# Attention products in one set of 512 columns a unit, key maxima turned in blocks, row sums moved by transfers

## The chip, the cores and the metric

The kernel runs on one core of one Trainium2 chip. The metric is the device time of one execution in microseconds (us). A core has TensorE (PE; its weight loads are shown as PEld), VectorE (DVE), ScalarE (ACT), GpSimd (POOL) and SyncE (SP), each with a program of its own; they meet at semaphores. SP, here, does little but start transfers (DMA); its queue is shown as SPq.

## The reference, cut to what matters

A macaron block on x of 8 x 512 x 128 values in float32: an attention and mixture-of-experts half, an RWKV-6 recurrence, and the same half again, each added to x.

```python
x = x + 0.5 * ffn(layernorm(x))     # "first mixer" and "first experts"
x = x + rwkv6(layernorm(x))
x = x + 0.5 * ffn(layernorm(x))     # "second mixer" and "second experts"

def ffn(x):                                            # 8 batches of 512 tokens, 128 channels
    h = layernorm(x) * w + b
    q, k, v = heads(h @ w_qkv)                         # 16 heads of 8 channels
    p = softmax(q @ k.T / sqrt(8))                     # 512 x 512 for every head and batch
    x = x + (p @ v) @ w_proj
    h2 = layernorm(x)
    return x + expert_mlp[argmax(h2 @ gate_w + gate_b)](h2)
```

The change lies in the attention and in the choice of the expert; the recurrence and the experts' own products are as they were.

## The kernel before, in words

`mixer_phase` does the attention half and the routing; it is called twice. For each of 8 batches `b` there are 4 steps `g` of four heads (a group), numbered G = 4 b + g. A step has 4 units `u` of 128 keys; 128 units in a mixer. A unit of group G holds:

- on TensorE four **scores** of group G + 2 (`score`, L652: queries in rows, all keys in 512 columns), from which VectorE takes the maxima over the keys;
- four **exponent products** of group G (`exponent`, L660: keys in rows, queries in columns; the maxima stand as extra rows of the stacked operand `q_stack`, so that the product comes out with the maximum taken off), which ScalarE turns into `probs` by Exp (L933);
- the **value products** of the unit before it (`pv`, L670: four matmuls of 32 output columns, one a head, side by side in the array; each over half of the 512 queries, so two sets of four a unit);
- and at some units one of the other jobs of a batch, by the rules of `jobs` (turning with the identity, the q, k and v projections, the output projection, the gate, the ranks).

Score and exponent product of one place are called a pair below; their operands lie in opposite halves of the array's rows. Two of TensorE's results go through small sets of PSUM banks: the scores through 4 banks (two pairs of heads; `reduce_pair`, L986, reads two banks at once and `s_read` frees them), the exponent products and all jobs in turn through a ring of 3 banks (`RINGS = 3`, `ring_free`: an instruction waits until the third user before it has been read). Every engine takes its instructions in the order written.

The maxima go from VectorE to GpSimd (`split_max`, split in a high and a low part), are turned by TensorE (`turn_max`, L679), copied by ScalarE (`keep_rows`), and written to the rows of `q_stack` by SP (`place`). The sums of the probabilities come out of the value products as a ninth column. At the end of two groups the sum bank is copied (`keep_o`), turned (`turn_o`), copied (`copy_o`), the sums inverted on VectorE (`invert`), multiplied on GpSimd (`normalize`), and the whole turned back once a batch (`turn_y`, `keep_y`) for `project`.

Before the first unit come the statistics, q, k and v of two batches, SP's stores of their split parts to memory and loads into the stacks of a group (12 transfers a group, `load_group`), and the scores of groups 0 and 1. After the last unit come the rest of the last batch's chain (output projection, norm, gate, rank, scatter of the rows to the experts' order) and 8 transfers of padding rows.

Of the kernel before, what the change touches and what calls it, by code (L numbers as in the profile page):

```python
# [5 lines left out]
F32 = mybir.dt.float32  # L6
# [186 lines left out]
def load_constants(nc, ctx, d, x_all, padding, xs):  # L193
# [14 lines left out]
    routing = [(sb("w_proj", [P, P]), d["L0_ffn_w_proj"]),  # L208
# [31 lines left out]

    def load_late(sp, part):
# [17 lines left out]
    with nc.Block() as block:  # L259
        @block.sync  # L260
        def _(sp):
            for dst, src in first:
                sp.dma_start(dst[:], src).then_inc(loaded, 16)
            for j in range(SL):
                here = slice(j * ST, (j + 1) * ST)
                sp.dma_start(x_all[:, here, :], x_slices[:, here, :]).then_inc(s["x_loaded"][j], 16)
            for dst, src in routing:
                sp.dma_start(dst[:], src).then_inc(s["routing_loaded"], 16)
# [14 lines left out]
    return s, load_late, wait_rest  # L283
# [14 lines left out]
def mixer_phase(nc, ps, s, x_all, z_all, rows, expert, first_row, xs, qd, kd, load=None):  # L298
    with Phase(nc) as ctx:
# [6 lines left out]
        def sbs(name, shape, dt=F32):  # L306
            return [sb(f"{name}{i}", shape, dt) for i in range(2)]

        y_all = rows[:, :, 0:P]
# [3 lines left out]
        spread, scales, power = sbs("spread", [P, 2, ST]), sbs("scales", [P, 2, ST]), sb("power", [P, 2, ST])  # L313
        zn, hT = sb("zn", [P, ST, P]), sb("hT", [P, SW])
# [9 lines left out]
        maxima = sbs("maxima", [P, 2, PAIRS, TPB])  # L324
        NMAX = 2 * SPLITS * PAIRS * TPB
        neg_wide = sb("neg_wide", [P, P], F32R)
        neg_parts = neg_wide[:, 0:NMAX].rearrange("p (e a m) -> p e a m", e=2, a=SPLITS)
        max_rows = sbs("max_rows", [P, P], F32R)
        oT = sb("oT", [P, T])
        o_rows, inv = sb("o_rows", [P, TPB, GROUP, SHARE, DK + 1]), sb("inv", [P, TPB, GROUP, SHARE])  # L330

        yT, h2T, x1 = sb("yT", [P, SW]), sb("h2T", [P, SW]), sb("x1", [P, ST, P])
# [15 lines left out]
            sem("power_set"), sem("ones_set"), sem("normed"), sem("z_made"), sem("turned"), sem("h_ready"))  # L348
        made = {k: sem(k + "_made") for k in "qkv"}
# [10 lines left out]
        split_step, split_done, rows_turned, rows_kept, rows_placed = (  # L360
            sem("split_step"), sem("split_done"), sem("rows_turned"), sem("rows_kept"), sem("rows_placed"))
        o_kept, o_turned, o_copied, inv_ready, o_done = (
            sem("o_kept"), sem("o_turned"), sem("o_copied"), sem("inv_ready"), sem("o_done"))

        numbered, y_turned, y_kept, projected = sem("numbered"), sem("y_turned"), sem("y_kept"), sem("projected")
# [5 lines left out]
        scattered, padded = sem("scattered"), sem("padded")  # L371
# [5 lines left out]
        PER_LOAD = 16 * 12  # L377
# [8 lines left out]
        def jobs(b, g, u):  # L386

            here = []
            if u == 1 and g % SHARE == 0 and (b or g):
                here.append(("o", shared(b, g)))  # L390
            if u == 1 and NG * b + g < LAST:
                here.append(("m", NG * b + g + 1))
            if b >= 2 and (g, u) == (0, 0):
                here.append(("gate", b - 2))
            if b >= 2 and (g, u) == (0, 2):
                here.append(("rank", b - 2))
            if b >= 1 and (g, u) == (1, 0):
                here.append(("turn_y", b - 1))
            if b + 2 < B and (g, u) == (1, 2):
                here.append(("turn_z", b + 2))  # L400
            if b >= 1 and (g, u) == (1, 3):
                here.append(("project", b - 1))
            if b + 2 < B and (g, u) == (2, 0):
                here.append(("q", b + 2))
            if b + 2 < B and (g, u) == (2, 2):
                here.append(("k", b + 2))
            if b >= 1 and (g, u) == (3, 0):
                here.append(("turn_h", b - 1))
            if b + 2 < B and (g, u) == (3, 2):
                here.append(("v", b + 2))  # L410
            if b == B - 1 and (g, u) == (3, 2):
# [1661 lines left out]
```

## Time and profile before

| | us |
|---|---|
| median of 3 runs (lowest, highest) | 1472.45 (1472.34, 1479.55) |
| the profiled execution: its time, its span | 1473.18, 1471.4 |
| TensorE busy over the span | 1230.9 (84%) |
| VectorE busy | 1042.9 (71%) |
| ScalarE busy | 860.7 (58%) |
| GpSimd busy | 553.6 (38%) |
| first mixer, from the first statistics to the experts' first load | 13.0 to 493.2 |

Busy time is the union of an engine's instructions. The profile shows the end of a matmul by a model, so two that follow each other overlap a little; the distance between starts is what a product costs the engine. A timeline row merges neighbouring instructions of one line: its first number is the start of the first, its second the time to the end of the last, xN their number (a matmul of float32 operands of L670, L699, L705 counts as two), and the bracket the idle time before it, with what ended it.

### The profile page before, as it was taken

How to read it: one execution, taken by the hardware profiler on the slowest of the kernel's cores; microseconds unless marked ns; L12 is line 12 of the kernel's file. 1: busy time of each engine (PE TensorE's matmuls, PEld its weight loads, DVE VectorE, ACT ScalarE, POOL GpSimd, SP SyncE). 2: the span in 40 equal slices, each digit the busy share in tenths (PEclk: the TensorE clock that was granted, in tenths of full speed). 3: DMA queues.
4: the chain of work that ended last, by engine and by line, in shares of the span. 5: the costliest groups of instructions: out<-in, count | busy, mean ns of one | idle time of the engine just before them, and what ended most of it. 6: DMA issues, size and time to landing. Idle time of an engine off the chain costs nothing. (4 is left out here: it accounts for less than half of the span.)

```text
span 1471.4 us, 36051 instructions
## 1 busy us (share of the span) xinstructions
PE 1230.9 (84%) x12512; PEld 661.3 (45%) x12513; DVE 1042.9 (71%) x1842; ACT 860.7 (58%) x1742; POOL 553.6 (38%) x797
## 2 busy tenths in 40 slices
PE   2799999999997596398888754999999999993893
PEld 1234444444443596145455442344444444442893
DVE  3889988988992332478788745888898988963232
ACT  2288877778775353444334411588788778881451
POOL 6122324323212354355676536222332431222462
PEclk9599999999999799599999955799999999996896
DMA  4322442222110121100000003122122122100224
GB/s 117 71 74 74 130 121 68 82 71 73 55 36 9 53 67 47 42 2 3 3 2 2 3 1 87 57 75 65 49 82 73 53 81 66 56 15 30 56 66 122
DMA packets 81540, 82.40 MB, mean 56 GB/s; under 512 B 16249, under 2 KB 53724, under 8 KB 81392
## 3 DMA queue, kind: packets, MB, share of 16 engines
q1 hardware_dynamic: 72560, 69.88, 16.7%
q0 software_dynamic: 4608, 8.44, 1.8%
q10 hardware_dynamic: 4224, 2.10, 0.5%
q8 instruction: 94, 1.54, 0.4%
q14 instruction: 54, 0.44, 0.1%
HBM read 50.42 MB, written 29.93 MB: 55 GB/s over the span
## 5 line engine op out<-in xcount | busy, mean ns | idle before, releaser
L986 DVE TENSOR_REDUCE maxima<-ps 128x2 f32<-128x1024 f32 x512 | 616.2, 1222 | 89.8 <-PE ps L652 88.5
L933 ACT ACTIVATE probs<-ps 128x512 f32<-128x512 f32 x1024 | 550.8, 600 | 120.3 <-PE ps L660 109.7
L652 PE MATMUL ps<-k_stack,q_stack 62*128 62x512 f32 x1024 | 390.0, 473 | 39.0 <-DVE maxima L986 21.7
L660 PE MATMUL ps<-q_stack,k_stack 64*128 64x512 f32 x1024 | 396.3, 464 | 4.2 <-ACT q_whole L869 3.4
L670 PE MATMUL ps<-probs,v_stack 128*32 128x256 f32 x4096 | 329.6, 394 | 0.9 <-ACT probs L933 0.4
L652 PEld LDWEIGHTS ps<-k_stack,q_stack 62*128 62x128 f32 x1024 | 160.1, 194 | 235.9 <-issue 138.3
L660 PEld LDWEIGHTS ps<-q_stack,k_stack 64*128 64x128 f32 x1024 | 159.2, 187 | 30.5 <-ACT q_whole L869 8.6
L670 PEld LDWEIGHTS ps<-probs,v_stack 128*32 128x32 f32 x4096 | 81.7, 108 | 166.6 <-issue 148.3
L532 POOL CAST neg_wide<-maxima 128x16 fp32r<-128x16 f32 x64 | 12.6, 196 | 286.7 <-DVE maxima L986 286.7
L1299 POOL DMA_INDIRECT expert_out<-yt,number x80 | 78.3, 979 | 72.4 <-POOL number L1295 44.1
L1276 DVE COPY w_now<-w 128x512 f32 x80 | 34.6, 433 | 80.1 <-issue 42.2
L1234 PE MATMUL ps<-xT,w_now 128*128 128x128 f32 x640 | 89.7, 285 | 0.2
L1241 PE MATMUL ps<-w,hidT 128*128 x640 | 84.7, 276 | 0.0
L1234 PEld LDWEIGHTS ps<-xT,w_now 128*128 128x128 f32 x640 | 80.9, 198 | 3.0 <-issue 2.4
L1257 ACT ACTIVATE xT<-ps,ln_b,ln_w 128x128 f32<-128x128 f32 x80 | 36.6, 457 | 73.1 <-PE ps L1228 73.1
L1241 PEld LDWEIGHTS ps<-w,hidT 128*128 128x128 f32 x640 | 78.2, 193 | 0.1
L558 POOL DMA_INDIRECT sorted<-rows,slot x64 | 63.6, 994 | 37.8 <-issue 20.8
L542 POOL TENSOR_TENSOR rows<-o_rows,inv 128x128 f32<-128x128 f32 x64 | 30.8, 501 | 122.1 <-DVE inv L993 122.1
L1262 ACT ACTIVATE hidT<-ps 128x512 f32<-128x512 f32 x80 | 47.8, 597 | 40.3 <-PE ps L1234 39.8
L1731 POOL TENSOR_TENSOR r_kx<-r_kx,r_k_factor 128x512 f32<-128x512 f32 x48 | 61.6, 1284 | 9.8 <-PE ps L1909 6.4
L1712 POOL TENSOR_TENSOR r_mixed<-r_shift,zT 128x512 f32<-128x512 f32 x40 | 58.7, 1474 | 16.0 <-DVE r_shift L1588 16.0
L1281 DVE COPY yt<-ps 128x128 f32<-128x128 f32 x80 | 23.3, 291 | 48.8 <-PE ps L1241 48.1
(208 smaller groups left out, 1622.7 us busy)
## 6 DMA issues: line engine op xcount, KB each, us to landing
q_stack<-q_split SPq DMA_DIRECT2D x256, 64.0 KB
k_stack<-k_split SPq DMA_DIRECT2D x512, 32.0 KB
q_split<-q_parts SPq DMA_DIRECT2D x16, 512.0 KB, 2.7
k_split<-k_parts SPq DMA_DIRECT2D x16, 512.0 KB, 3.6
xt<-sorted SPq DMA_DIRECT2D x80, 64.5 KB
w<-in_L_ffn_w SPq DMA_DIRECT2D x16, 256.0 KB, 3.0
rows<-expert_out SPq DMA_DIRECT2D x16, 256.0 KB, 4.5
x_all<-in_L_attn_x SPq DMA_DIRECT2D x8, 256.0 KB, 5.1
```

The lines of the kernel that those rows point to most:

```text
L558: pool.indirect_dma_start(xs, bass.IndirectOffsetOnAxis(ap=slot[:, i:i + 1], axis=0), rows[:, i, :], None).then_inc(scattered, 16)
L652: mm = t.matmul(psS[:, h, :], qs[g][score_rows(h), h // 2, u * P:(u + 1) * P], ks[g][score_rows(h), h // 2, :], start=True, stop=True)
L660: t.matmul(ring("e", G, u, n), ks[G % NG][half(h), h // 2, u * P:(u + 1) * P], qs[G % NG][half(h), h // 2, :], start=True, stop=True).then ...
L670: last = t.matmul(psO[VW * h:VW * (h + 1), here], vs[g][:, u, h, :], probs[u % 2][:, h, here], start=(g % SHARE == 0 and u == 0 and part = ...
L933: a.activation(probs[u % 2][:, h, :], ring("e", G, u, n), ACT.Exp, scale=float(DK) ** -0.5).then_inc(e_read, 1)
L986: v.tensor_reduce(maxima[G % 2][:, :, pair, u:u + 1], psS[:, 2 * pair:2 * pair + 2, :], AX_X, ALU.max, negate=True).then_inc(s_read, 1)
L1234: last = t.matmul(psH[o][:, c * P:(c + 1) * P], w1_now[o][:, c * P:(c + 1) * P], xT[o][:], start=True, stop=True)
L1241: last = t.matmul(psY[i][:, 0:P], hidT[i][:, c, :], s["w2"][:, ds(second_expert, 1), c, :], start=(c == 0), stop=(c == HC - 1))
L1262: a.activation(hidT[o][:].rearrange("p c t -> p (c t)"), psH[o], ACT.Gelu_apprx_tanh).then_inc(hidT_kept, 1)
L1299: pool.indirect_dma_start(ys, bass.IndirectOffsetOnAxis(ap=number[out_slot][:], axis=0), yt[out_slot][:], None, bounds_check=TOK - 1, oob_ ...
L1712: g.tensor_tensor(mixed[f][:], shift[f % 2][:], x, ALU.add).then_inc(mixed_ready.sem, 1)
L1731: g.tensor_tensor(dst[:].rearrange("p (k m) -> p k m", m=m), src[:].rearrange("p (k m) -> p k m", m=m), k_factor[l][:].rearrange("p n two ...
```

## The change

**Value products.** One set of four matmuls over all 512 queries, behind all four pairs of the unit, in place of two sets of 256 behind two pairs each.

**Maxima.** VectorE turns the 128 x 32 maxima in 32 x 32 blocks itself (`turn_maxima`); GpSimd splits the result; SP writes two images to memory and reads them back into `q_stack`. `turn_max` and `keep_rows` are gone from TensorE and ScalarE.

**Sums.** `oT` keeps the value products as they come. SP moves the sum rows to a 128 x 32 tile, VectorE inverts them, SP writes them to memory and reads them back repeated over the rows (`inv_wide`), GpSimd multiplies. `turn_o`, `copy_o`, `turn_y`, `keep_y` are gone; `project` runs over two halves of rows, 8 matmuls in place of 4.

**Norms.** The first norm's second scaling and the row norm move from VectorE to ScalarE in two units each (with scale and bias); `halve` moves from VectorE to GpSimd; the latter's 4 scalings become 2 operations over 512 columns.

**Transfers.** 4 loads a group of 32 rows in place of 12; q and k are stored in four transfers in place of two (the same parts twice). In the first mixer only two slices of x are loaded ahead, the rest and the routing constants from inside the phase. The padding rows go half from SP, half from ScalarE.

**Places.** The jobs stand at other units (`jobs`), and the last batch but one's gate and rank come behind the last unit.

```diff
 def jobs(b, g, u):
-    if u == 1 and g % SHARE == 0 and (b or g):
-        here.append(("o", shared(b, g)))
-    if u == 1 and NG * b + g < LAST:
-        here.append(("m", NG * b + g + 1))
-    if b >= 2 and (g, u) == (0, 0):
+    if b >= 2 and (g, u) == (0, 1):
+        here.append(("turn_h", b - 2))
+    if b >= 2 and (g, u) == (0, 3):
         here.append(("gate", b - 2))
...
+AFTER = [(k, B - 2) for k in ("turn_h", "gate", "rank")] + [(k, B - 1) for k in ("project", "turn_h", "gate", "rank")]
...
-def pv(unit, part):
+def pv(unit):
     g, u = unit // TPB % NG, unit % TPB
-    if part == 0:
-        pe.wait_ge(e_read, 4 * unit + 4)
-    here = slice(part * T // 2, (part + 1) * T // 2)
+    pe.wait_ge(e_read, 4 * unit + 4)
     for h in range(GROUP):
-        last = t.matmul(psO[VW * h:VW * (h + 1), here], vs[g][:, u, h, :], probs[u % 2][:, h, here],
+        last = t.matmul(psO[VW * h:VW * (h + 1), :], vs[g][:, u, h, :], probs[u % 2][:, h, :],
...
-                        if ahead:
-                            score(G + 2, u, 0)
-                        exponent(G, u, 0)
...
-                        values(1)
+                        for n in range(GROUP):
+                            if ahead:
+                                score(G + 2, u, n)
+                            exponent(G, u, n)
...
+                        if unit:
+                            pv(unit - 1)
...
 def project(p):
+    pe.wait_ge(o_done, NG // SHARE * (p + 1))
     for q in range(ST):
+        for n in range(NG // SHARE):
+            last = t.matmul(ring("project", p)[:, q * P:(q + 1) * P], yT[n][:, q * P:(q + 1) * P], s["w_proj"][:, n, :],
+                            start=(n == 0), stop=(n == NG // SHARE - 1))
...
+def turn_maxima(G):                       # VectorE
+    v.transpose(max_turned[:], maxima_wide[G % 2][:]).then_inc(max_blocks, 1)
...
+def place(G):                             # SP
+    image = max_images[G % 2]
+    for a, ready in enumerate((split_step, split_done)):
+        sp.wait_ge(ready, G + 1)
+        sp.dma_start(image[a].rearrange("c k q -> k c q"), neg_parts[:, a, :].bitcast(F32)).then_inc(max_stored, 16)
+    sp.wait_ge(max_stored, STORED * (G + 1))
+    for e in range(2):
+        sp.dma_start(qs[G % NG][at:at + SPLITS, :, :].bitcast(F32),
+                     image[:, e * count:(e + 1) * count]).then_inc(rows_placed, 16)
...
+def move_sums(count):                     # SP
+    sp.wait_ge(o_kept, count)
+    sp.dma_start(sums[:], oT[DK::OW, :]).then_inc(sums_moved, 16)
+def store_inv(count):
+    sp.wait_ge(inv_ready, count)
+    sp.dma_start(inv_image.rearrange("r (k q) -> (r k) q", q=BLOCK), inv[:]).then_inc(inv_stored, 16)
+def spread_inv(count):
+    sp.wait_ge(inv_stored, 16 * count)
+    sp.dma_start(inv_wide[:], inv_image.unsqueeze(1).broadcast_to([P // OW, OW, T])).then_inc(inv_spread, 16)
...
+def norm_second(j, tiles):                # ScalarE; norm_rows likewise, at (3, 2) and (3, 3)
+    for q in tiles:
+        last = a.activation(zn[:, q, :], x_all[:, j * ST + q, :], ACT.Identity, bias=shift[j % 2][:, q:q + 1],
+                            scale=scales[j % 2][:, 1, q:q + 1])
...
-for e in range(E):
+for e in range(E // 2):                   # padding rows on SP; the other half on ScalarE
```

On TensorE, one whole unit before, in the middle of the first mixer (L652 is a score, L660 an exponent product, L670 the value products of the unit before; a job, where there is one, follows the last row):

```order
L652 MATMUL ps<-k_stack_175,q_stack_171 128x512
L660 MATMUL ps<-q_stack_169,k_stack_173 128x512
L652 MATMUL ps<-k_stack_175,q_stack_171 128x512
L660 MATMUL ps<-q_stack_169,k_stack_173 128x512
L670 MATMUL ps<-probs_181,v_stack_177 32x256 x4
L652 MATMUL ps<-k_stack_175,q_stack_171 128x512
L660 MATMUL ps<-q_stack_169,k_stack_173 128x512
L652 MATMUL ps<-k_stack_175,q_stack_171 128x512
L660 MATMUL ps<-q_stack_169,k_stack_173 128x512
L670 MATMUL ps<-probs_181,v_stack_177 32x256 x4
```

Two pairs are followed by one set over 256 columns, twice. On TensorE after the change, a whole unit in the first mixer (L697 is a score, L705 an exponent product, L713 the value products):

```order
L697 MATMUL ps<-k_stack_169,q_stack_165 128x512
L705 MATMUL ps<-q_stack_163,k_stack_167 128x512
L697 MATMUL ps<-k_stack_169,q_stack_165 128x512
L705 MATMUL ps<-q_stack_163,k_stack_167 128x512
L697 MATMUL ps<-k_stack_169,q_stack_165 128x512
L705 MATMUL ps<-q_stack_163,k_stack_167 128x512
L697 MATMUL ps<-k_stack_169,q_stack_165 128x512
L705 MATMUL ps<-q_stack_163,k_stack_167 128x512
L713 MATMUL ps<-probs_174,v_stack_171 32x512 x4
```

The four pairs now stand without the value products between the second and the third, and the set is 512 columns wide. On TensorE behind the last unit of the first mixer, before (L685 turns the sum bank, L713 turns the attention's rows back, L722 is the output projection, L730 turns the normed rows, L737 is the gate):

```order
L670 MATMUL ps<-probs_181,v_stack_179 32x256 x8
L685 MATMUL ps<-ident,oT 128x128 x4
L713 MATMUL ps<-ident,rows 128x128 x4
L722 MATMUL ps<-w_proj,yT 128x128 x4
L730 MATMUL ps<-ident,rows 128x128 x4
L737 MATMUL ps<-gate_w,h2T 128x8 x4
```

and after (L772 ends the rank of batch 6, L746 is the output projection of batch 7 in its two halves, L754 the turn of its normed rows):

```order
L772 MATMUL ps<-one_hot,ones_narrow 128x8
L746 MATMUL ps<-w_proj,yT_187 128x128
L746 MATMUL ps<-w_proj,yT_188 128x128
L746 MATMUL ps<-w_proj,yT_187 128x128
L746 MATMUL ps<-w_proj,yT_188 128x128
L754 MATMUL ps<-ident,rows 128x128 x4
```

Both turns ahead of the projection are gone there; what the projection waits for now comes through SP's three transfers.

## Rows read from the trace of the kernel before

**Rows 1.** Busy time of each engine over full units of the first mixer.

```profile
80.00:440.00 360.00, 352.34 (x3084) 153.26 (x3077) 319.55 (x474) 287.89 (x559) 103.42 (x178) 1.00 0.27 79
```

**Rows 2.** TensorE's timeline over one unit without a job.

```profile
208.78 0.50 PE L652 MATMUL ps<-k_stack,q_stack 62*128 62x512 f32 x1
...
209.44 0.64 PE L670 MATMUL ps<-probs,v_stack 128*32 128x256 f32 x8
210.00 0.50 PE L652 MATMUL ps<-k_stack,q_stack 62*128 62x512 f32 x1
...
211.23 0.50 PE L652 MATMUL ps<-k_stack,q_stack 62*128 62x512 f32 x1
```

**Rows 3.** TensorE's timeline: a q projection, and the v projections of neighbouring batches.

```profile
135.19 1.12 PE L699 MATMUL ps<-hT,w_qkv 128*128 128x512 f32 x2
...
155.48 1.16 PE L705 MATMUL ps<-w_qkv,hT 128*128 128x128 f32 x8
...
207.69 1.16 PE L705 MATMUL ps<-w_qkv,hT 128*128 128x128 f32 x8
```

**Rows 4.** TensorE's timeline where three pairs stand together, then one.

```profile
162.46 0.73 PE L660 MATMUL ps<-q_stack,k_stack 64*128 64x512 f32 x2
...
163.37 0.64 PE L670 MATMUL ps<-probs,v_stack 128*32 128x256 f32 x8
163.94 0.50 PE L660 MATMUL ps<-q_stack,k_stack 64*128 64x512 f32 x1
164.37 0.64 PE L670 MATMUL ps<-probs,v_stack 128*32 128x256 f32 x8
```

**Rows 5.** Timeline near the end, where no scores are left.

```profile
449.60 0.50 PE L660 MATMUL ps<-q_stack,k_stack 64*128 64x512 f32 x2
...
450.13 2.09 ACT L933 ACTIVATE probs<-ps 128x512 f32<-128x512 f32 x4 [0.16 <-PE ps L660]
...
450.60 0.68 PE L660 MATMUL ps<-q_stack,k_stack 64*128 64x512 f32 x2
```

**Rows 6.** TensorE's groups by line, 100 to 400 us (jobs that change).

```profile
L685 PE MATMUL ps<-ident,oT 128*128 128x128 f32 x48 | 7.9, 286 | 0.0
L679 PE MATMUL ps<-ident,neg_wide 128*128 128x128 f32 x24 | 7.2, 301 | 0.0
L722 PE MATMUL ps<-w_proj,yT 128*128 128x128 f32 x48 | 7.0, 288 | 0.0
```

**Rows 7.** ScalarE's group of one copy; VectorE's timeline around a choice.

```profile
L859 ACT ACTIVATE hT<-ps,ln_b,ln_w 128x512 f32<-128x512 f32 x5 | 3.9, 778 | 1.5 <-PE ps L692 1.5
...
162.57 0.19 DVE L1055 TENSOR_TENSOR logit<-ps,gate_b 128x32 f32<-128x32 f32 x1 [0.33 <-PE ps L737]
...
164.19 2.34 DVE L986 TENSOR_REDUCE maxima<-ps 128x2 f32<-128x1024 f32 x2
```

**Rows 8.** Timeline of the first mixer's head.

```profile
13.01 0.87 DVE L950 BATCH_NORM_STATS2 stats<-x_all 128x6 f32<-128x128 f32 x4 [8.19 <-PEq L259]
...
29.86 0.33 SPq L458 DMA_DIRECT2D q_stack<-q_split  x1
...
37.19 1.22 PE L652 MATMUL ps<-k_stack,q_stack 62*128 62x512 f32 x4 [7.77 <-DMA k_stack<-k_split]
...
49.25 9.14 DVE L986 TENSOR_REDUCE maxima<-ps 128x2 f32<-128x1024 f32 x8 [2.09 <-PE ps L652]
```

**Rows 9.** Timeline behind the first mixer's last unit.

```profile
463.32 0.60 ACT L845 ACTIVATE oT<-ps 128x512 f32<-128x512 f32 x1 [1.19 <-PE ps L670]
...
468.93 0.69 DVE L1018 TENSOR_TENSOR x<-z_all,ps 128x512 f32<-128x512 f32 x1 [3.47 <-PE ps L722]
...
481.32 8.46 SPq L496 DMA_DIRECT2D sorted<-padding  x8
```

**Rows 10.** Transfers by issue: KB each, median us from issue to landing.

```profile
w<-in_L_ffn_w SPq DMA_DIRECT2D x16, 256.0 KB, 3.0
...
sorted<-padding SPq DMA_DIRECT2D x16, 64.5 KB, 2.2
```

More of the change, by code:

```diff
@@ L473, in _ @@
+                if load is not None:
+                    load[0](sp)
+                store_q(0)
+                store_k(0)
                 for g in range(NG):
                     load_group(0, g)
-                store(1, "q", qd)
-                store(1, "k", kd)
+                store_q(1)
+                store_k(1)
                 place(0)
@@ L707, in value @@
                     last.then_inc(made["v"], 1)
-                def turn_y(p):
-                    pe.wait_ge(o_done, NG // SHARE * (p + 1))
-                    ring_free("turn_y", p)
-                    for q in range(ST):
-                        last = t.transpose(ring("turn_y", p)[:, q * P:(q + 1) * P], rows[:, p * ST + q, 0:P], s["ident"][:])
-                    last.then_inc(y_turned, 1)
                 def project(p):
@@ L936, in _ @@
                 for kind, j in AFTER:
+                    if (kind, j) == ("turn_h", B - 1):
+                        norm_rows(j, range(ST))
                     job(kind, j)
+                act.wait_ge(pads_ready, 1)
+                for e in range(E // 2, E):
+                    row = act.value_load(pad_row[0:1, e:e + 1], min_val=0, max_val=E * (TOK + P) - P)
+                    act.dma_start(xs[ds(row, P), :], s["padding"][:, 0, :]).then_inc(act_padded, 16)
+                act.wait_ge(act_padded, 16 * (E - E // 2))
             @block.vector
@@ L1090, in _ @@
                 for j in range(2):
-                    norm_both(j, range(ST))
+                    norm_second(j)
+                for k in "qk":
+                    low_part(0, k)
                 for i in range(2):
@@ L1134, in _ @@
-                        if (b, g, u) == (0, 3, 0):
+                            if (u, pair) == (0, 0) and G < LAST:
+                                turn_maxima(G + 1)
+                        if u == 0 and g % SHARE and G > 1:
+                            invert(shared(b, g - 1))
+                        if (g, u) == (0, 3) and b >= 2:
+                            choose(b - 2, b + 2 if b + 2 < B else None)
+                        if (g, u) == (0, 3) and b < 2:
+                            stats_of(b + 2, range(ST))
@@ new lines, in _ @@
+                        if (g, u) == (1, 0) and b + 2 < B:
+                            moments_of(b + 2)
+                        if (g, u) == (2, 1) and b >= 1:
+                            add(b - 1)
+                        if (g, u) == (2, 3) and b >= 2:
+                            places(b - 2, b - 1)
+                        if (g, u) == (2, 3) and b == 1:
+                            row_stats(0, range(ST))
+                        if (g, u) == (3, 0) and b >= 1:
+                            row_moments(b - 1)
```

454 lines of the change are left out of this document (204 added, 250 removed).

## The prediction

> **What bounds the kernel now.** I read the busy times first. Over the full units of the first mixer TensorE is busy for 352.3 of 360 us, VectorE for 319.6, ScalarE for 287.9 [rows 1]. The two mixers are over half of the time, so a unit's length there, times 256, is what the change acts on. The timeline of TensorE shows what a unit consists of: the next unit starts 2.45 us after this one (211.23 less 208.78), each half being 0.66 of two pairs and 0.57 of value products [rows 2]. VectorE needs two reductions of 1.14 a unit when it never waits (9.14 for 8) [rows 8], 2.28 in all; it is next, but not the bound of a unit without a job. A job stands behind a unit and adds its own length; with jobs and waits a batch of 16 units lasts 52.2 us, from one v projection to the next (207.69 less 155.48) [rows 3], where 16 bare units would take 39.2.
>
> What the busy share hides is a delay that is not long enough to matter yet. Near the end, where there are no scores, an exponent product starts at 449.60, ScalarE takes it up at 450.13, and the third user of the ring behind it starts at 450.78 (the end of the two at 450.60, 451.28, less the 0.50 of one) [rows 5]: **a bank of the ring comes back 1.18 us after its product started**, 0.53 to ScalarE, 0.60 of Exp, 0.05 back. Four exponent products on three banks: the fourth of a unit can't start before the first plus 1.18. Before the change it starts at about 1.56, since a set of value products lies between; so nobody waits.
>
> **The change, part by part.**
>
> *The order of the unit.* Two pairs take 0.66 [rows 2], three take 0.91 (162.46 to 163.37), a lone one 0.43 (163.94 to 164.37) [rows 4]: every further pair 0.24, so four would take 1.15 and the fourth would start at 0.82. It has to wait until 1.18. Being alone then, it takes 0.42 to the value products, which start at 1.60.
>
> *The wider set.* No row shows four matmuls of 32 columns over 512. A set over 256 costs 0.57 [rows 2]. Twice that, 1.14, is the upper bound. A single product over 512 columns costs 1.05 (1.12 busy less the overlap of 0.07 that L670 has too, 0.64 against 0.57) [rows 3], with four times the weights to load. For the lower bound: the v projection streams the same 512 columns in four pieces for 1.09 (1.16 less 0.07) [rows 3], so three more starts cost 0.04 in all; a start cannot be worth much more than the 0.19 by which a lone pair exceeds the 0.24 of a further one [rows 4]; 1.14 less 0.19 is 0.95. I take 1.00, between 0.95 and 1.05.
>
> The unit is then 1.60 + 1.00 = **2.60 us against 2.45, 0.15 longer**, though TensorE's own work in it falls to 2.15. VectorE's 2.28 fits.
>
> The Trainium skill says in TensorEngine Tiling (Array Packing), Key Properties, that changing the tiling mode drains the array. By that rule two changes of mode fewer a unit are pure gain, and the unit would fall towards 2.15. The rows of a lone pair agree that such a drain has a price; the rule says nothing of the ring.
>
> *Jobs on TensorE, a batch.* Gone are four turns of the maxima (7.2/24 = 0.30 each), two of the sums (7.9/12 = 0.66) and one of the rows (of the same size), 3.2 us busy, some 2.6 of engine time with 0.07 off each; the projection doubles, +1.1 (7.0/6) [rows 6]. Net -1.5.
>
> *Waits, a batch.* The copy of a turned or projected job stands on ScalarE ahead of the unit's first Exp. A copy of 0.78 [rows 7] makes that Exp start at 0.8 in place of 0.53; the q and k jobs have two copies. Before, 1.56 less 1.18 = 0.38 of slack took most of this; now it moves the fourth product itself: two turns at 0.27, q and k at 0.5, v 0.1, about 1.6, some 1.3 of it new. The two halves of a norm that ScalarE takes over at four units fall into its idle time of 0.8 between the last Exp of a unit and the first of the next. A wait goes as well: in the second unit of a step three pairs stood together today and the third waited for VectorE, 0.2 each. Choice and places behind gate and rank block VectorE as before (162.57 to 164.19) [rows 7]. Net +0.7.
>
> A batch: 16 x 0.15 - 1.5 + 0.7 = **+1.6**, 53.8 us. Seven such batches +11; the last 8 units, where ScalarE's four Exps (2.09 + 0.16) set 2.25 today [rows 5], rise to 2.60, +2.8; gate, rank and turn of batch 6 leave the units, -2. So +12 a mixer, **+24** in all.
>
> *Head.* In the first mixer VectorE starts at 13.01 because SP first issues 8 slices and 8 constants [rows 8]; with two slices it starts when these land, near 6.2: -6.8, once. In both mixers: the loads of the first group take 7.3 us from 29.86 to the scores at 37.19 [rows 8], most of it the issue of 12 transfers at 0.33; four take 1.3 to issue and then, as now, some 3 to 3.5 to land: 4.8, -2.5. The stores carry twice the bytes but start 1.3 to 2.4 earlier, since VectorE sets the constants of the stacks behind them: -1. Between the scores of groups 0 and 1 VectorE waits 2.09 for the turn of the maxima [rows 8], gone: -2.1. Together -6.8 - 2 x 5.6 = **-18**.
>
> *Tail.* From the copy of the sum bank (463.32) to the sum of attention and input (468.93) are 5.6 us [rows 9]. Now: copy 0.6; a transfer, 2.2, the inverse 0.4, a transfer, 2.2, one of 256 KB, 3.0 [rows 10]; the product on GpSimd 1.4; eight cold projections, 3.5 as an estimate from twice 1.17 and the slower clock. 13.4, +7.8. ScalarE's four scalings and GpSimd's extra shift, +0.9. The padding takes 8.46 us of SP's queue [rows 9]; half of it goes away, -4.0, as the last scatter then ends at about the same time. Net +4.7, **+9.4** for two.
>
> *Maxima.* They are due a whole step later, 13 us. VectorE turns them in the first unit (2 us), GpSimd splits (0.6), two transfers out and two back (5.5): 8 to 9. The fullest step of GpSimd (by its groups in the same stretch: split, row scale, two low parts 2.7, four scatters 5.2, `halve` 2.7) runs about 2.5 into the next and still leaves some 2. Cost 0, with this cover.
>
> **Sum.** 24 - 18 + 9 = +15 on the profiled 1473.2 (span 1471.4 and 1.8 around it), 1488.6. The median of the runs stands 0.7 below the profiled time: **1488 us**.
>
> **The rivals.**
>
> *The ring does not hold the fourth product (faster).* If the bank comes back by 0.82 instead of 1.18, VectorE's 2.28 is the unit: -0.17 for 240 units, -41, jobs -1.5 for 14 batches, -21, half of it lost again to VectorE's jobs; with head and tail -9: about 1415 to 1430. It decides as soon as the release falls under about 1.03 us. Against it stands that 1.18 was read with ScalarE otherwise idle; for it, that only one place of the trace shows it. By the skill's rule above alone this would be the result.
>
> *No change.* The wider set costs 0.90 and copies hide: the unit is 2.50, steady part +6, head and tail -9: 1466 to 1479.
>
> *The maxima come late (slower still).* If images and reads back take 3 us more than I sum in the step behind GpSimd's fullest, TensorE waits there: 3 us in each of 6 batches of both mixers, +36: about 1525. It decides from 2 us more on. For it: a store that has to be seen in memory before the read back is not in the trace.
>
> **Chances.** Forecast 0.55 (its own range 1474 to 1506), faster rival 0.12, no change 0.18, late maxima 0.15. The range to hold the time 8 times in 10 takes in no change and the lower part of the late maxima and the bounds of the set (0.05 x 256 = 13 on either side): 1462 to 1514. A difference of 0.5%, 7 us, is about what a measurement of this kernel can tell. Faster by more (the faster rival, and half of no change): 0.20. Within: 0.19. Slower: 0.61.
>
> **What would show it.** A bare unit of TensorE at 2.60, with its fourth exponent product 1.18 behind the first and a wait there on ScalarE's Exp; the set of value products 1.00 from start to start; batches of 53.8; VectorE's idle time before the reductions larger than today; the add of the last batch 13 behind the copy of the sum bank; the head shorter by 12 in the first mixer and 5.6 in the second. The prediction is wrong if the fourth product starts with the third, or if pairs wait for `rows_placed` at the start of a step.

## The result and the profile after

The changed kernel takes 1527.63 us (1524.48 to 1530.64, 4 runs) against 1472.39 for the kernel before in the same session: a ratio of 1.0364, with a 95% interval of 1.0324 to 1.0404. The forecast was 1488 with a range to 1514. The direction was right, and the size was not: +15 forecast, +55 measured.

The changed kernel's page, engines and two costly groups (line, names, count | busy us, mean ns | idle before, and its releaser):

```profile
PE 1233.9 (81%) x10336; PEld 650.0 (43%) x10337; DVE 998.3 (65%) x1814; ACT 847.0 (55%) x1742; POOL 584.1 (38%) x797
...
L926 ACT ACTIVATE probs<-ps 128x512 f32<-128x512 f32 x1024 | 530.4, 608 | 167.4 <-PE ps L705 165.3
L705 PE MATMUL ps<-q_stack,k_stack 64*128 64x512 f32 x1024 | 403.2, 467 | 48.5 <-ACT probs L926 39.4
```

L697 is now the score, L705 the exponent product, L713 the value products, L926 the Exp. TensorE waits 39.4 us ahead of exponent products for an Exp. Not all of that is the ring alone: in a_two below, where one other wait is taken out, it is 19.7. The windows view (busy us of each engine, then the clock) for the stretch of [rows 1]:

```profile
80.00:440.00 360.00, 332.20 (x1959) 139.41 (x1958) 276.97 (x432) 261.61 (x518) 110.41 (x167) 0.99 0.37 107
```

TensorE, VectorE and ScalarE are all busy for less of it than before (352.3, 319.6 and 287.9 there), GpSimd for a little more; what was added is waiting, not work. TensorE's timeline over a bare unit and the one behind it, to be held against [rows 2]:

```profile
151.10 0.50 PE L697 MATMUL ps<-k_stack,q_stack 62*128 62x512 f32 x1
151.10 0.73 PE L705 MATMUL ps<-q_stack,k_stack 64*128 64x512 f32 x2
...
152.29 0.49 PE L705 MATMUL ps<-q_stack,k_stack 64*128 64x512 f32 x1
152.71 1.06 PE L713 MATMUL ps<-probs,v_stack 128*32 128x512 f32 x8
153.71 0.50 PE L697 MATMUL ps<-k_stack,q_stack 62*128 62x512 f32 x1
...
156.29 0.50 PE L705 MATMUL ps<-q_stack,k_stack 64*128 64x512 f32 x1 [1.19 <-ACT probs L926]
156.72 1.93 PE L713 MATMUL ps<-probs,v_stack 128*32 128x512 f32 x8
```

The first unit is the forecast to the last step: the fourth exponent product 1.19 behind the first (152.29 less 151.10), the value products 0.42 later, 1.00 from their start to the next unit, 2.61 in all. The unit behind it holds what was not forecast. Its fourth exponent product comes 2.58 behind its first. ScalarE's timeline says why:

```profile
155.15 0.60 ACT L838 ACTIVATE oT<-ps 128x512 f32<-128x512 f32 x1 [1.45 <-POOL yT L592]
155.65 2.06 ACT L926 ACTIVATE probs<-ps 128x512 f32<-128x512 f32 x4
```

and GpSimd's in the same place:

```profile
145.97 1.27 POOL L564 TENSOR_TENSOR x_all<-x_all,half_x 128x512 f32<-128x512 f32 x1
153.28 0.21 POOL L582 CAST neg_parts<-max_turned 128x32 fp32r<-128x32 f32 x1 [6.04 <-DVE max_turned L994]
...
153.78 1.28 POOL L592 TENSOR_TENSOR yT<-oT,inv_wide 128x512 f32<-128x512 f32 x1
```

`keep_o` (L838, on ScalarE) copies the sum bank into `oT`. There is one `oT`, and `normalize` (L592, on GpSimd) of the count before must have read it. SP issued the read of the inverse into `inv_wide` at 144.15; with the 4.2 us that such a read takes to its use (below, a_half_two_tail) `normalize` could have run at about 148, an estimate. But GpSimd's program has `split_max` ahead of it, and that waits for VectorE's maxima until 153.28. So ScalarE stands still for 1.45 us with four Exps queued behind the copy, TensorE waits for those, and behind the wait TensorE's granted clock falls from 1.00 to 0.50, 2.4 to 1.2 GHz, for about 3 us. By windows of one microsecond:

```profile
155.00:156.00 1.00, 0.10 (x1) 0.00 (x0) 1.00 (x2) 0.85 (x2) 0.32 (x2) 1.00 1.10 232
156.00:157.00 1.00, 0.71 (x5) 0.38 (x9) 0.84 (x1) 1.00 (x3) 0.00 (x0) 0.89 0.91 275
157.00:158.00 1.00, 1.00 (x8) 0.00 (x0) 0.00 (x0) 0.71 (x2) 0.00 (x0) 0.50 0.22 42
...
159.00:160.00 1.00, 1.00 (x6) 0.67 (x6) 0.00 (x0) 0.27 (x1) 0.00 (x0) 0.50 0.06 16
```

The value products at 156.72 take 1.93 in place of 1.06. Such a fall of the clock stands at two more places of the first mixer (102 and 382), each behind a `keep_o`. It is not the rule: TensorE stands idle for 1.17 to 1.22 us at 16 copies of the sum bank, eight in each mixer, and behind the other 13 the clock stays at 1.00. The copy's own line, over the whole kernel:

```profile
L838 ACT ACTIVATE oT<-ps x32: 587/597/599, 73.9 to 1376.1; 128x512 f32<-128x512 f32 x32
its engine sat idle before it (us, times) until:
  POOL yT L592: 27.5, 18
```

Sixteen of the 18 are these, 1.45 us each; the other two, 2.1 each, are the last copies of the mixers and belong to their tails.

**The account.** The stretch of the Exps, from the start of a mixer's first to the start of its last, and what lies between, in us of the profiled executions:

| stretch | before | after | difference | forecast |
|---|---|---|---|---|
| head of the first mixer | 58.2 | 46.4 | -11.8 | -12.4 |
| Exps, first mixer | 403.3 | 427.7 | +24.4 | +12 |
| last Exp to the experts' first load | 31.6 | 43.8 | +12.2 | +4.7 |
| experts' first load to the second mixer's first Exp | 435.2 | 432.0 | -3.2 | -5.6 |
| Exps, second mixer | 401.8 | 423.4 | +21.6 | +12 |
| last Exp to the end | 141.3 | 153.9 | +12.6 | +4.7 |
| span | 1471.4 | 1527.2 | +55.8 | +15 |

So of the 40 us by which the forecast fell short, 37 have two addresses: the steady part, 22 more than forecast, and the tails, 15 more. The fourth row is the least certain: the experts and the recurrence in it have the same program in every kernel here, and the time from the experts' first load to VectorE's first statistics of the second mixer is 390.1 before and 391.2 after, and lies between 387.7 and 392.3 in other runs of this record.

### The profile page after: what moved, and what is told of

It reads as the page before. It is cut to its first block and busy times, and to the rows that moved or that the text cites. A ratio compares the mean times of both kernels' runs of the same rounds, so it can differ in the third digit from the quotient of the medians.

```text
span 1527.2 us, 31409 instructions
## 1 busy us (share of the span) xinstructions
PE 1233.9 (81%) x10336; PEld 650.0 (43%) x10337; DVE 998.3 (65%) x1814; ACT 847.0 (55%) x1742; POOL 584.1 (38%) x797
## 5 line engine op out<-in xcount | busy, mean ns | idle before, releaser
L986 DVE TENSOR_REDUCE maxima<-ps 128x2 f32<-128x1024 f32 x512 | 606.0, 1216 | 141.9 <-PE ps L697 141.1
L926 ACT ACTIVATE probs<-ps 128x512 f32<-128x512 f32 x1024 | 530.4, 608 | 167.4 <-PE ps L705 165.3
L705 PE MATMUL ps<-q_stack,k_stack 64*128 64x512 f32 x1024 | 403.2, 467 | 48.5 <-ACT probs L926 39.4
L697 PE MATMUL ps<-k_stack,q_stack 62*128 62x512 f32 x1024 | 347.3, 456 | 41.6 <-DVE maxima L986 30.1
L713 PE MATMUL ps<-probs,v_stack 128*32 128x512 f32 x2048 | 276.5, 612 | 0.0
L697 PEld LDWEIGHTS ps<-k_stack,q_stack 62*128 62x128 f32 x1024 | 167.1, 196 | 250.1 <-DVE maxima L986 169.0
L705 PEld LDWEIGHTS ps<-q_stack,k_stack 64*128 64x128 f32 x1024 | 167.5, 187 | 167.9 <-ACT probs L926 129.5
L582 POOL CAST neg_parts<-max_turned 128x32 fp32r<-128x32 f32 x64 | 13.4, 209 | 554.9 <-DVE max_turned L994 554.9
L713 PEld LDWEIGHTS ps<-probs,v_stack 128*32 128x32 f32 x2048 | 40.5, 108 | 66.8 <-ACT probs L926 37.7
L1639 DVE TENSOR_TENSOR r_qx<-r_qx,r_q_factor 128x512 f32<-128x512 f32 x48 | 56.6, 1179 | 0.1
```

Source lines behind the costliest of these rows:

```text
L697: mm = t.matmul(psS[:, h, :], qs[g][score_rows(h), h // 2, u * P:(u + 1) * P], ks[g][score_rows(h), h // 2, :], start=True, stop=True)
L705: t.matmul(ring("e", G, u, n), ks[G % NG][half(h), h // 2, u * P:(u + 1) * P], qs[G % NG][half(h), h // 2, :], start=True, stop=True).then ...
L713: last = t.matmul(psO[VW * h:VW * (h + 1), :], vs[g][:, u, h, :], probs[u % 2][:, h, :], start=(g % SHARE == 0 and u == 0), stop=(g % SHAR ...
L926: a.activation(probs[u % 2][:, h, :], ring("e", G, u, n), ACT.Exp, scale=float(DK) ** -0.5).then_inc(e_read, 1)
L986: v.tensor_reduce(maxima[G % 2][:, :, pair, u:u + 1], psS[:, 2 * pair:2 * pair + 2, :], AX_X, ALU.max, negate=True).then_inc(s_read, 1)
L1639: v.tensor_tensor(dst[:].rearrange("p (k m) -> p k m", m=m), src[:].rearrange("p (k m) -> p k m", m=m), q_factor[l][:].rearrange("p n two ...
```

## The experiments

Two theories had to be told apart for the steady part: that the wide set costs more than its unit shows (the ring, with the copies and jobs), or that the wait of `keep_o` is a cost of its own.

**a_half: the changed kernel with the value products in two sets of 256 again.**

```diff
-                        if unit:
-                            pv(unit - 1)
+                            if n == (2 if u == 1 else 1):
+                                values(0)
+                        values(1)
```

> The changed kernel with the value products again in two sets of 256 columns, behind the second and the fourth pair (behind the third and the fourth in the second unit of a step); all else as changed. Theory of the ring (four exponent products between two sets on three banks hold the fourth): a bare unit of 2.61 us goes back to 2.46, and about 240 units give back 30 to 36 us: 1527 to some 1494. Rival (the sums' new path alone makes the loss, the width is immaterial): 1520 to 1530, with the unit's other waits grown in its place.

Measured: 1498.42, ratio 1.0159 (1.0126 to 1.0192). These runs and the next three stood beside a kernel before of 1476.44; the later ones beside 1474.35 or 1474.88. The changed kernel itself was timed only beside 1472.39, so a difference between runs of two sessions can be off by some 4 us. A bare unit is back at 2.47 (from 101.61), and the gain of 29 is at the low end of the forecast 30 to 36. Without the wide set the changed kernel is still 22 us slower than the one before.

**b_wide: the kernel before with the wide set alone**, the mirror of that diff.

> The kernel before with nothing changed but the value products in one set over 512 columns behind the four pairs. Theory of the ring: bare unit 2.60 in place of 2.45, a wait of the fourth exponent product on the Exp of the first, 1472 to 1500 or 1505. Rival (fewer changes of the array's tiling, TensorE's own work in a unit 0.3 less): 1472 or less.

Measured: 1500.82, ratio 1.0174 (1.0144 to 1.0203). Its Exps last 415.2 and 415.1 us, +11.9 and +13.3. In the timeline the same unit stands as in the changed kernel, 2.61 us (211.53 less 208.92), with the fourth product 1.19 behind the first:

```profile
208.92 0.73 PE L660 MATMUL ps<-q_stack,k_stack 64*128 64x512 f32 x2
...
210.11 0.50 PE L660 MATMUL ps<-q_stack,k_stack 64*128 64x512 f32 x1
210.53 1.07 PE L668 MATMUL ps<-probs,v_stack 128*32 128x512 f32 x8
211.53 0.38 PE L702 MATMUL ps<-w_qkv,hT 128*128 128x128 f32 x1
```

**a_two: the changed kernel with two buffers of oT**, so that `keep_o` waits for the `normalize` of two counts ago.

```diff
-                    if count >= 2:
-                        act.wait_ge(o_done, count - 1)
-                    a.activation(oT[:], psO, ACT.Copy).then_inc(o_kept, 1)
+                    if count >= 3:
+                        act.wait_ge(o_done, count - 2)
+                    a.activation(oT[count % 2][:], psO, ACT.Copy).then_inc(o_kept, 1)
```

> The changed kernel with two buffers for the copy of the sum bank, so that the copy no longer waits for GpSimd to have multiplied the one before it; all else as changed. Theory (this wait stands in ScalarE's queue ahead of four Exps, once in two steps, and is the part of the steady loss that I did not forecast): ScalarE's 27.5 us of waiting for that product go, the dips of TensorE's clock at those places too, 1527 to 1500 or 1507. Rival (the time is absorbed, the unit is set by other waits): 1520 or more.

Measured: 1498.32, ratio 1.0147 (1.0119 to 1.0176). Exps of 414.3 and 412.2 us. The copy's line now reads:

```profile
L838 ACT ACTIVATE oT<-ps x32: 587/597/599, 73.9 to 1347.1; 128x512 f32<-128x512 f32 x32
its engine sat idle before it (us, times) until:
  PE ps L713: 2.4, 2
```

and the exponent products' on its page, against 39.4 in the changed kernel:

```profile
L705 PE MATMUL ps<-q_stack,k_stack 64*128 64x512 f32 x1024 | 402.1, 466 | 28.9 <-ACT probs L926 19.7
```

ScalarE's 27.5 us of waiting for `normalize` are gone, TensorE's wait for Exps is shorter by 19.7 (16 times 1.2 is 19), and the time falls by 29. Of the 29, the two stretches of Exps account for 13.4 and 11.2; some 3 lie between the mixers, in the experts and the recurrence (391.2 and 387.8), which the edit doesn't touch. The falls of the clock at the three copies are gone too, as expected; one stands at 115.5 instead, behind no such wait.

**a_half_two: both.**

> Both edits: two sets of 256 columns and two buffers for the copy of the sum bank. If the two causes are separate, their gains add: about 1527 - 33 - 23 = 1471. If they cover each other, no less than 1485.

Measured: 1465.15, ratio 0.9919 (0.989 to 0.9948): 0.8% faster than before. The two causes are separate: 29.2 and 29.3 us alone, 62.5 together, 4 more than their sum. In the stretches of Exps alone it is 28 and 25, and 58 together, 5 more. Its windows row for the stretch of [rows 1] has TensorE busy again:

```profile
80.00:440.00 360.00, 350.04 (x3060) 149.44 (x3056) 296.09 (x466) 291.05 (x565) 116.08 (x177) 1.00 0.39 109
```

**a_order and a_half_order: the order of GpSimd's program in place of a second buffer.**

```diff
-                    if G < LAST:
-                        split_max(G + 1)
                     if g % SHARE == 0 and G > SHARE:
                         normalize(shared(b, g) - 1)
+                    if G < LAST:
+                        split_max(G + 1)
```

> The changed kernel with one buffer of oT as it is, and only GpSimd's program changed: normalize of the previous count stands ahead of the step's split_max, not behind it. In the trace GpSimd stands idle for 6.0 us ahead of that split, while the inverse has long been spread. Theory (ScalarE's copy of the sum bank waited because normalize stood behind a split that waits for VectorE's maxima): as with two buffers, 1498, between 1493 and 1504. Rival (what helped was the second buffer, and a normalize that waits for a transfer now holds back the maxima): 1515 to 1535.

> Two sets of 256 in their old places and normalize ahead of split_max: both causes cured without a second buffer. Theory: 1465, between 1460 and 1470, as with the second buffer. Rival as above: 1480 to 1498.

Measured: 1506.51, ratio 1.0211 (1.0186 to 1.0237), and 1477.93, ratio 1.0022 (1.0006 to 1.0037). Both lie between the two forecasts: 21 us of the 29 come back in the first, and each stands above its kernel with two buffers, by 8 and 13 us. The rest of the wait is in the copy's line of a_order:

```profile
  POOL yT L592: 10.6, 12
```

and in GpSimd's timeline of a_order the reason:

```profile
172.18 1.28 POOL L592 TENSOR_TENSOR yT<-oT,inv_wide 128x512 f32<-128x512 f32 x1 [2.50 <-DMA inv_wide<-inv_image]
```

Where `normalize` no longer waits for the split, it waits for the transfer itself (70.6 us in 18 waits), and at 12 counts that is still too late for the copy. So the place behind `split_max` is most of this cause, the length of the path by memory the rest, and of the kernels run here only those with the second buffer cover both.

**a_ring2 and b_ring2: a ring of two banks in place of three, after and before.**

```diff
-RINGS, FIRST_RING = 3, 4
+RINGS, FIRST_RING = 2, 4
```

> The changed kernel with a ring of two banks in place of three for exponent products and jobs. Theory: a bank comes back 1.18 us after its product started, so the third of a unit waits for the first and the fourth for the second: fourth at 1.51, value products at 1.84 to 1.93, a bare unit of 2.84 to 2.93 in place of 2.61. Rival (ring not the limit of a unit): 2.61 stays. The whole time is of less use, since jobs take ring places too.

> The kernel before with a ring of two banks. Theory: in a bare unit the third product starts 1.23 behind the first, later than 1.18, so the unit stays at 2.46; units with three pairs together and those behind a job grow, so the whole time grows by some tens of us. Rival (a ring that is smaller costs the same in both orders): a bare unit longer by 0.2 to 0.3.

One run each: 1657.92 and 1594.98 us. The second is 120 us above the kernel before, not the "some tens" of the expectation. A bare unit of a_ring2 in TensorE's timeline:

```profile
180.10 0.49 PE L705 MATMUL ps<-q_stack,k_stack 64*128 64x512 f32 x1
...
181.29 0.50 PE L705 MATMUL ps<-q_stack,k_stack 64*128 64x512 f32 x1
...
181.78 0.49 PE L705 MATMUL ps<-q_stack,k_stack 64*128 64x512 f32 x1
183.19 0.50 PE L697 MATMUL ps<-k_stack,q_stack 62*128 62x512 f32 x1
```

Now the **third** product stands 1.19 behind the first. The fourth stands 1.68 behind it, since the second's Exp queues on ScalarE behind the first's (0.53 + 0.60 + 0.60 = 1.73), and the unit is 3.1, longer than I had expected since I had left that queue out; no unit without a job is shorter in the middle of the first mixer. In b_ring2 the same limit is seen, where it was not expected either:

```profile
159.93 0.73 PE L660 MATMUL ps<-q_stack,k_stack 64*128 64x512 f32 x2
...
161.60 0.49 PE L660 MATMUL ps<-q_stack,k_stack 64*128 64x512 f32 x1
...
162.59 0.50 PE L652 MATMUL ps<-k_stack,q_stack 62*128 62x512 f32 x1
```

Its fourth product is held until 1.67 behind the first, and the unit is 2.66 (162.59 less 159.93), not the 2.46 that I had expected to stay. It is no single case: the shortest units without a job in the first mixer of b_ring2 take 2.67, so the rival's 0.2 to 0.3 came out for this kernel, while the changed one pays 0.5. The depth of the ring is what ties the products to the Exps.

**a_two_short and a_half_two_short: a shorter Exp.** Every Exp reads and writes 256 of its 512 columns, TensorE's program unchanged; the other half of the probabilities is a constant, so these kernels leave work out and their outputs are not the reference's. This shortens the return of a bank, and ScalarE's share of a unit with it (four Exps in 1.36 us in place of 2.06).

```diff
-                            a.activation(probs[u % 2][:, h, :], ring("e", G, u, n), ACT.Exp,
+                            a.activation(probs[u % 2][:, h, 0:T // 2], ring("e", G, u, n)[:, 0:T // 2], ACT.Exp,
```

> The changed kernel with oT in two buffers (1498 us), and with every Exp over the first 256 of its 512 columns only; the other half of the probabilities holds a constant 1.0, set once by GpSimd in the head (some 2 us a mixer), so the outputs are not the reference's. TensorE's program is the same to the instruction. By the nearest row, a copy of 288 columns by ScalarE at 0.41 against 0.60 for 512, the Exp falls to about 0.39 and the return of a bank from 1.18 to about 0.97. Theory (the fourth exponent product waits for the ring, and the set of value products only makes that wait visible): the unit falls from 2.60 to 0.97 + 0.42 + 1.00 = 2.39, and the time by 16 x 0.21 x 16 = 54, less what VectorE's 2.28 and its jobs take back: 1440 to 1460. Rival (the wide set itself is what costs, by its own length or by its reloading of weights): the fourth product does not move, 1490 to 1500.

> The same short Exp (outputs not the reference's, as above) in the kernel with two sets of 256 and two buffers of oT (1465 us), as the control: here the fourth product of a bare unit doesn't wait, so only units behind a job gain, at most 1.6 a batch or 25 in all, and VectorE is near: 1445 to 1465. Theory: the wide set, 33 us dearer than two narrow ones with the full Exp, is then no dearer, since its unit is 2.39 against 2.46; the difference of the two kernels is between -15 and +5. Rival (the wide set itself costs): the difference stays near +33.

Measured: 1454.69, ratio 0.9859 (0.984 to 0.9878), and 1450.87, ratio 0.9832 (0.9813 to 0.9852). The wide set was 33 us dearer with the full Exp (1498.3 against 1465.2) and is 4 dearer with the short one. The bare unit of a_two_short:

```profile
151.04 0.49 PE L707 MATMUL ps<-q_stack,k_stack 64*128 64x512 f32 x1
...
152.03 0.50 PE L707 MATMUL ps<-q_stack,k_stack 64*128 64x512 f32 x1
152.46 1.07 PE L715 MATMUL ps<-probs,v_stack 128*32 128x512 f32 x8
153.45 1.06 PE L763 MATMUL ps<-gate_w,h2T 128*128 128x8 f32 x8
```

The fourth product is 0.99 behind the first (forecast 0.97, with an Exp that measures 0.383), and the unit 2.41 (forecast 2.39). The wide set costs 0.99 still. In a_half_two_short the shortest bare units are 2.45, as with the full Exp. So it is the wait on the ring that makes the wide set a loss.

**a_half_two_tail: the last normalize ahead of the scatter of batch 6.**

```diff
                 normalize(NG * B // SHARE - 1)
-                scatter(B - 2)
                 normalize(NG * B // SHARE)
+                scatter(B - 2)
```

> The changed kernel with two sets of 256 columns, two buffers for the copy of the sum bank, and in GpSimd's program the last product with the inverse sums ahead of the scatter of batch 6 in place of behind it. In the trace after, the four scatters end 2.1 us after the repeated inverse can have landed, in each mixer; but the scatters then stand ahead of the row scale of the last batch, 5.1 us of GpSimd against 3.8 of projections and 2 of VectorE's work. Theory: 2 us a mixer, 1465 to 1461. Rival (GpSimd's work is only shifted): no difference.

Measured: 1464.76, ratio 0.9934 (0.9915 to 0.9954), no difference from a_half_two. GpSimd's row there:

```profile
454.51 1.26 POOL L592 TENSOR_TENSOR yT<-oT,inv_wide 128x512 f32<-128x512 f32 x1 [8.80 <-DMA inv_wide<-inv_image]
```

against 455.12 in a_half_two. SP issued the read at 450.30 here and at 450.00 there, so the product comes 4.2 behind it in place of 5.1: having the scatter ahead costs 0.9 us, not the 2 of the theory; the rest is a wait for the transfer that is there without it.

**a_pads: all eight padding transfers on SP again.**

> The changed kernel with all eight transfers of padding rows on SP, as before the change; all else as changed. My forecast had taken 4 us a mixer for this edit. Theory now: the end of a mixer waits for the landing of GpSimd's last scatter, some 6 us behind its issue, in both kernels, and the padding is covered: 1527, a difference under 2. Rival (the padding rules): 1535.

Measured: 1526.55, ratio 1.0355 (1.0337 to 1.0374), the changed kernel's time. SP's queue in it:

```profile
505.27 8.14 SPq L532 DMA_DIRECT2D sorted<-padding  x8
517.01 6.84 SPq L1200 DMA_DIRECT2D xt<-sorted  x6
```

The padding is issued until 513.41 in place of 509.25, and yet the time is the same. What ends the wait is in the landings. The last padding transfer of a_pads, issued at 513.08, and the last scatter of the changed kernel, issued at 509.09, with the time from issue to landing at the end:

```profile
sorted<-padding SPq DMA_DIRECT2D x1, 64.5 KB, 1.9
```

```profile
sorted<-rows,slot POOLq DMA_INDIRECT x1, 4.2
```

In a_pads the experts' first load, at 517.01, starts 2.0 us behind the landing of that padding (515.0). The distance is 2.0 to 2.1 in both mixers of all four kernels that have eight on SP, the kernel before among them. In the changed kernel the load, at 518.07, starts 4.75 behind the landing of that scatter, and the distance is 4.7 to 4.8 in both mixers of all ten kernels that split the padding. In a_pads the last scatter landed 3.1 behind its issue, at 511.9; with 4.7 behind it the load would have started only 0.4 earlier (0.9 in the second mixer). So with eight on SP the padding does end last, against the theory that it is covered, but by less than 1 us in a_pads (for the kernel before the scatter's landing is not in the trace); and with the split the scatter lands later, 4.2 and 4.7 behind its issue. Splitting the padding between two queues saves nothing.

**The tail, read.** The changed kernel's SP, GpSimd and VectorE behind the first mixer's last unit, against [rows 9]; first GpSimd's timeline:

```profile
486.52 0.96 POOL L607 DMA_INDIRECT sorted<-rows,slot  x1 [0.30 <-issue]
487.50 1.27 POOL L592 TENSOR_TENSOR yT<-oT,inv_wide 128x512 f32<-128x512 f32 x1
...
509.09 0.96 POOL L607 DMA_INDIRECT sorted<-rows,slot  x1 [0.30 <-issue]
```

then SP's queue and VectorE:

```profile
477.56 0.62 SPq L484 DMA_DIRECT2D sums<-oT  x1
480.95 0.34 SPq L490 DMA_DIRECT2D inv_image<-inv  x1
482.39 0.60 SPq L494 DMA_DIRECT2D inv_wide<-inv_image  x1
505.56 3.69 SPq L532 DMA_DIRECT2D sorted<-padding  x4
```

```profile
492.65 0.69 DVE L1024 TENSOR_TENSOR x<-z_all,ps 128x512 f32<-128x512 f32 x1 [10.77 <-PE ps L746]
```

The copy stands at 476.94, held for 2.15 by the `normalize` of the count before; before the change it waited for 1.19, for TensorE [rows 9]. The add comes 15.7 behind it, against 5.6 before [rows 9]. The scatter of batch 6 ends its issue just ahead of the product at 487.50; the last scatter is issued by 510.05, and the experts' first load starts 8.0 later, at 518.07; SP's padding was issued by 509.25 already.

## Why the prediction was wrong, point by point

**The unit and the ring: right.** The return of 1.18 us, read at one place where ScalarE was idle, holds as 1.19 in the changed kernel, in b_wide and, for the third product, in a_ring2; shortening the Exp by 0.22 shortened it by 0.20. The set of four over 512 queries measures 1.00, the value taken between 0.95 and 1.05; the unit 2.61 against 2.60. The faster rival falls with it. That the release decides is borne out, but not that 1.03 us is enough: with the return at 0.99 the wide set is still not faster than the narrow one, 4 us dearer. On the side of the rule of the Trainium skill (TensorEngine Tiling (Array Packing), Key Properties, that changing the tiling mode drains the array) stands the 0.14 that one set of 1.00 saves on two of 0.57; whether that is the drain, or the starts of four matmuls that are saved, is not shown. The time did not fall by it, even with the return of 0.99.

**The steady part: the term comes out, in part by luck, and one is missing.** Forecast +24 for both mixers. With the wait of `keep_o` taken out (a_two) the Exps take 414.3 and 412.2, +21.4 over before. The working was a little off on the way: a full batch takes 54.5 there, not 53.8, against 52.2 before, and the first and the seventh batch are no longer than before, where the forecast had +1.6 for each.

The missing term is that wait: 13.4 and 11.2 us in the two stretches, which brings a full batch to 55.8. The step of the prediction that failed is "Waits, a batch": it listed the copies of turned and projected jobs by what their length adds ahead of an Exp (0.27, 0.5, 0.1), left the copy of the sum bank out, and never asked what a copy waits for. Before, that copy's destination was read by TensorE's turns, and the copy waited for TensorE alone, 2.4 us in all. The change made its destination the operand of GpSimd's `normalize`, which waits for three transfers and an inverse of VectorE, and stands in GpSimd's program behind `split_max`, which waits for VectorE's maxima. The prediction's own working followed `normalize` in the tail only. In the steady part the wait holds ScalarE 16 times for 1.45 and TensorE 16 times for 1.2, 19 us; the three times that the clock fell, all in the first mixer, fit its stretch losing 2.2 more than the second. In a_order, with waits of 10.6, the clock stayed at 1.00 over the stretch of 75 to 440.

**The size of the steady part by experiment.** The wide set alone costs 24 us on the kernel before, 29 on the changed one and 33 where `keep_o` doesn't wait. The forecast's 0.15 for each of 256 units is 38. That a bare unit pays it in full is shown, and a full batch of 16 units pays 2.1 on the kernel before (54.3 against 52.2) and 2.8 with two buffers (54.5 against 51.7), about the 2.4 of the forecast; the first batches and the last ones pay less, which of their units is not shown.

**The tail: wrong by 7.5 a mixer.** The largest part is a saving of 4.0 for the padding that does not exist: with four transfers on SP or with eight the time is the same (a_pads). The prediction took the end of SP's issue for the end of the mixer. By the landings the padding did end last before the change, but another wait, the scatter's landing and 4.7 us behind it, ends almost as late (0.4 and 0.9 earlier in a_pads), and the split moved that landing later: the experts' first load comes 8.0 behind the last scatter's issue in place of 7.4 (before: 485.8 to 493.2). Then the chain from the copy to the add was 15.7 in place of 13.4, 2.3 more, and the copy itself came 1.0 later behind the start of the last Exp (2.8 in place of 1.8). By a_half_two_tail, where nothing stands ahead of it, the read of `inv_wide` is 4.2 from issue to use (450.30 to 454.51), not 3.0, and in the changed kernel the scatter of batch 6 adds 0.9; the move of the sums with the inverse is 3.4 (477.56 to 480.95) and not 2.6; the store is the only one that was shorter, 1.4 in place of 2.2. The projection takes 3.78, against 3.5.

**The head: 1.2 too much in each mixer.** From VectorE's first statistics to the first Exp it is 40.7 in both mixers, against 45.2 and 45.1 before: 4.5 and 4.4 less, where 5.6 was forecast. In the first mixer VectorE also started 7.4 earlier (5.66 against 13.01) and not 6.8, so that its sum of -11.8 comes nearer to -12.4 than its parts. The term that was wrong is the stores of q and k: they start 2.3 earlier, but from the first one's issue to the first load of a stack it is 7.0 us (16.15 to 23.16) in place of 4.1 (25.81 to 29.86), a loss of 0.6 in place of a gain of 1. The loads gain 3.1, the maxima 2.1, as forecast or better. The other 1.2 by which the second mixer's row falls short lies in the experts and the recurrence.

**The maxima: right.** No pair waits for `rows_placed` at a step's start, so the "late maxima" rival did not come about, though the time lay near its 1525. That nearness is chance: the wait that cost the time is on ScalarE, for GpSimd, and not on TensorE for SP.

**In sum:** -15 (head) + 21 (steady, without the wait) + 25 (the wait) + 25 (tails) = +56, where the forecast had -18 + 24 + 0 + 9.

## What to carry to other kernels

For each instruction that is left in place, ask what its destination is now read by. A copy that gets a new reader inherits that reader's place in another engine's program, with everything that stands ahead of it there: here one buffer more was worth 29 us (25 of them in the stretches it acts on) and an exchange of two lines 21. A slack (0.38 us of ring time here) can be used up by a mere change of order: write the return time of a ring down next to the distance of its users before merging two products into one. And what is taken off a queue's issue saves at most the distance to the next landing that the stage behind waits for: 4 us of issue were worth nothing here, since another wait ended less than 1 us before.

## What the runs showed of the hardware

In the changed kernel TensorE waited for 1.17 to 1.22 us at 16 copies of the sum bank, each time in a unit that had been busy. Three of these waits were followed by a stretch of about 3 us at a granted clock of 0.50, in which a set of value products took 1.93 in place of 1.06, and 13 by none. In a_half four of 16 waits of 0.96 to 1.45 were. In a_two the clock fell once (at 115.5) where TensorE had had no idle time over 0.41 in the 5 us before. What decides it I leave open.

With eight padding transfers on SP the experts' first load came 7.2 to 7.8 us behind the end of the issue of the last indirect scatter, with the padding split between two queues 8.0 to 9.3; behind the landing of that scatter it came 4.7 to 4.8 us later in every kernel with the split. Which of the steps behind the landing take these 4.7 us the traces don't show. A store and the read back of a row of inverses took 1.4 us from issue to issue and 4.2 from issue to use, so a round trip by memory of 16 KB out and 256 KB in stands at 5.6 us.
